# An earlier or later place for the time kernel's turns, the expert loads, the rank products and the token list of a two-layer mixture kernel

## The chip, the cores and the metric

One core of a Trainium2 chip runs the kernel. The metric is the device time of one execution in microseconds; each version is run several times, and the median is given. The engines are TensorE (PE; PEld is its weight load), VectorE (DVE), ScalarE (ACT), GpSimd (POOL) and SyncE (SP), which here only issues loads and stores. DMA is the 16 engines that move the data.

## What is computed

The input `x` is 32 x 32 x 512, that is 1,024 tokens of 512 numbers, in f32. There are two layers, each with a residual:

```python
x = x + ffn0(mix0(x))       # mix0: 32x32 channel matrix, picked per batch entry from 16
x = x + ffn1(conv1(x))      # conv1: a long convolution per channel, masked by length

def ffn0(xt):               # 16 experts, 2 per token, and a shared one of twice the width
    scores = softmax(xt @ router_w + router_b) + router_bias
    ...                     # best 2 of 4 groups, then best 2 experts
    y = sum over experts of gate * ((silu(xt @ ew1 + eb1) * (xt @ ew2 + eb2)) @ ew3 + eb3)
    z = (silu(xt @ sw1 + sb1) * (xt @ sw2 + sb2)) @ sw3 + sb3
    return y + z

def conv1(u):               # the kernel of 512 taps per channel comes from log_dt, C, A
    K = 2 * Re(Cs @ exp(dtA * arange(512)))
    ...
def ffn1(h):                # relu(h @ up)**2 @ down, plus a latent path scaled by the top-2 gate logits
    ...                     # (h @ fc1) @ expert_w, times the sum of the two best logits, @ fc2
    return layernorm(...)
```

The change lies in the first layer, before its expert blocks. Two things of the second layer are prepared there: the rows from which the convolution's kernel (the time kernel) is made, and `expert_w`, turned by TensorE into `ewt`.

## The kernel before

The kernel is written engine by engine; each engine's instructions run in the order written, and semaphores join them. Products that need f32 accuracy are made of three fp32r products of high and low parts (`split3`, L413 to L420): `ah` and `al` hold the mixed tokens, `swh` and `swl` the shared expert's weights.

**Mixing** (PE L1395 to L1413). For each of 8 tiles of 128 tokens PE makes a mixing product, ACT copies it to `xstage` (L692, and every second tile it issues a store to `xrow` in DRAM), PE turns it (L1371), ACT copies the turned tile to `ah` (L734) and DVE the rest to `al` (L919). From tile 4 on, every second tile, PE adds a piece of the router's logits (L1389). Ahead of product 2 PE makes four small turns of the time kernel's rows (L1399, into bank 7), which wait for `s4_in`, four small loads of which `sdt` is the last; they raise `tr_done`. ACT in the same loop takes the exponential of `sdt` (L725, at i == 0) and copies and exponentiates the turned rows (L729 and L732, at i == 1). POOL waits for these, makes five small steps, and then casts the second half of the shared weights (L587, `split_hi(1)`), which DVE splits later (L915).

**Loads** (SP L445 to L486). SP issues in order the tokens, the small loads, the shared weights, then, after `tr_done`, `ewraw` (`expert_w`; it lies where the time kernel's rows lay), and the weights of eight experts (`static_pair` 0 to 3: three loads of 512 KB each, twelve in all). A further pair and `fcraw`, `fc2raw` follow when the mixing is over and `xrow` is stored.

**Shared products and routing** (PE L1502 to L1535). PE makes eight shared products of 12 matmuls each, in four pairs. After pair 0 it waits for `ewraw`, turns it (L1511), and waits until ACT has copied it to `ewt`. Meanwhile DVE works out the routing mask from the logits (L936 to L966). Before the second product of pair 1 the rank products (L1448, L1449) wait for that mask. DVE then works out each token's place in an expert's block and from that two sets of one-hot rows, `hotb` and `hotp` (L1031 to L1037). The last shared product (L1468) is interleaved with 24 small list products of them (L1474, L1477), two behind each of its 12 matmuls; the first 16 give the tokens of each block (`tokx`, L1052), the other 8 their places. POOL gathers the blocks' tokens with them (L622).

**Blocks.** After eight products for a bias (`b3_term`) the 31 expert blocks follow: turn the gathered tokens (L1525), two products with the expert's weights (L1561), one back (L1531). Behind them come the combination, the convolution and the second layer.

Of the kernel before, what the change touches and what calls it, by code (L numbers as in the profile page):

```python
# [27 lines left out]
P = 128  # L28
# [10 lines left out]
def adaln_ffn_program(nc, x, cond, length, cond_w, router_w, router_b, router_bias, ew1, eb1, ew2, eb2, ew3, eb3,  # L39
# [4 lines left out]
    NT = N // P  # L44
    KC = T // P
    BT = P // C
    HALF = N // 2
    TH = NT // 2
    E, _, INTER = ew1.shape
    SH = sw1.shape[1] // INTER  # L50
    G = SH + E
    K = 2
# [22 lines left out]
    YS = 4  # L75
    HOLD = 3
    WARM = 2
    XGS = 4
    AHEAD = 7
    YOS = 4  # L80
# [10 lines left out]
    CBANK = (7, 0, 1, 6)  # L91
# [30 lines left out]
    ah = at(main, "ah", [P, KC, N], F32R)  # L122
    al = at(main, "al", [P, KC, N], F32R)
# [6 lines left out]
    swh = at(exp_reg, "swh", [P, 2, SCOLS], F32R)  # L130
    swl = at(exp_reg, "swl", [P, 2, SCOLS], F32R)
# [181 lines left out]
    bank = [nc.alloc_psum_tensor(f"bank{i}", [P, 512], F32) for i in range(8)]  # L313
# [10 lines left out]
    st_in = [sem(f"st_in{k}") for k in range(4)]  # L324
# [4 lines left out]
    wraw_in, wall_done, wbd2_ok = sem("wraw_in"), sem("wall_done"), sem("wbd2_ok")  # L329
# [21 lines left out]
    a_done, c_done, y_done = sem("a_done"), sem("c_done"), sem("y_done")  # L351
# [8 lines left out]
    b12_ok, ewt_ok = sem("b12_ok"), sem("ewt_ok")  # L360
# [52 lines left out]
    def split3(pe, dst, lhs, rhs, n_k, start=True, stop=True):  # L413

        for k in range(n_k):
            (lh, ll), (rh, rl) = lhs(k), rhs(k)
            pe.matmul(dst, lh, rh, start=(start and k == 0), stop=False)  # L417
            pe.matmul(dst, lh, rl, start=False, stop=False)  # L418
            mm = pe.matmul(dst, ll, rh, start=False, stop=(stop and k == n_k - 1))  # L419
        return mm  # L420
# [20 lines left out]
    def _(sp):  # L441
# [27 lines left out]
        def static_pair(g, landed):  # L469

            dst = ew[:, 2 * g:2 * g + 2, :]
            for src, col in ((ew1, W1), (ew2, W2)):
                sp.dma_start(dst[:, :, col:col + KC * P],
                             src[2 * g:2 * g + 2].rearrange("e (p k) m -> p e (k m)", p=P)).then_inc(landed, 16)
            sp.dma_start(dst[:, :, W3], ew3[2 * g:2 * g + 2].rearrange("e p n -> p e n")).then_inc(landed, 16)

        sp.wait_ge(tr_done, 1)
        sp.dma_start(ewraw[:, :, :], expert_w.rearrange("(a p) m -> p a m", p=P)).then_inc(ew_in, 16)
        for g in range(4):
            static_pair(g, st_in[g // 2])  # L480
        sp.wait_ge(mix_done, NT)
        for par in range(2):
            sp.wait_ge(xrow_out[par], 16 * NT // 4)
# [29 lines left out]
        for n in range(NB):  # L513
# [9 lines left out]
            if n in TOEP_STEPS:  # L523
                g = TOEP_STEPS.index(n)
# [154 lines left out]
    def _(act):  # L679
# [38 lines left out]
        for i in range(NT):  # L718
            if i + 1 < NT:
                x_row(i + 1)  # L720
            if i == 0:
                act.wait_ge(s4_in, 64)
                for a in range(2):
                    s = slice(a * HN, (a + 1) * HN)
                    act.activation(sw[s, 1, :], sdt[s, a::2], ACT.Exp).then_inc(exps_ok, 1)  # L725
            if i == 1:

                act.wait_ge(tr_done, 1)
                act.activation(spar[:, :, :], bank[7][:, 0:4 * HT].rearrange("p (k h) -> p k h", k=4), ACT.Copy)\  # L729
                    .then_inc(spar_ok, 1)  # L730
                act.wait_ge(spar_ok, 1)
                act.activation(sw[:, 0, :], spar[:, 0, :], ACT.Exp).then_inc(exps_ok, 1)  # L732
            act.wait_ge(mix_done, i + 1)
            act.activation(ah[:, :, i * P:(i + 1) * P], bank[2 * (i % 3)][:, :].rearrange("p (k n) -> p k n", k=KC), ACT.Copy)\  # L734
                .then_inc(ah_ok, 1)
            if i >= 4 and i % 2 == 0:
                ltr_copy(i // 2 - 2)
# [615 lines left out]
    def _(pe):  # L1353
# [7 lines left out]
        for w in (6, 7):  # L1361
            for b in range(BT):
                mm = pe.matmul(bank[w][b * C:(b + 1) * C, :], ident[0:C, 0:C],
                               wraw[:, :, :].rearrange("c k d -> c (k d)"), start=True, stop=True)
# [26 lines left out]
            mm.then_inc(lgt_done, 1)  # L1391

        for i in range(NT):
            if i == 2:

                pe.wait_ge(wbd2_ok, BT * len(ACT_TILES))
                pe.wait_ge(s4_in, 64)
                for k, src in enumerate((sstage[:, 0, :], sstage[:, 1, :], cstage[:, :, 0], cstage[:, :, 1])):
                    mm = pe.transpose(bank[7][:, k * HT:(k + 1) * HT], src, ident[0:HT, 0:HT])  # L1399
                mm.then_inc(tr_done, 1)  # L1400
            if i in ACT_TILES:
                pe.wait_ge(wbd2_ok, BT * (ACT_TILES.index(i) + 1))
            else:
                pe.wait_ge(wbd_ok, 1 + BT * (DVE_TILES.index(i) + 1))
            pe.wait_ge(x_in[i // 2], 16)
            wait(pe, xst_ok, i - 2)
            pe.matmul(bank[2 * (i % 3) + 1][:, :], wbd[:, i, :], acc[:, i, :], start=True, stop=True)\  # L1407
                .then_inc(mixr_done, 1)
            if i:
                transpose_mixed(i - 1)  # L1410
            if i >= 4 and i % 2 == 0:
                router_logits(i // 2 - 2)
# [4 lines left out]
        for k in range(2):  # L1417
            mm = pe.transpose(bank[3][:, k * G:(k + 1) * G], bstage[:, k, :], ident[0:G, 0:G])
# [24 lines left out]
        def rank_products():  # L1443

            pe.wait_ge(const_ok, TRI)
            pe.wait_ge(msk_ok, 1)
            wm = w2t[:, :, :].rearrange("p i e -> p (i e)")
            pe.matmul(bank[2][:, 0:NT * E], tri[:, :], wm, start=True, stop=True)  # L1448
            pe.matmul(bank[2][:, NT * E:2 * NT * E], ones[:, :], wm, start=True, stop=True).then_inc(rank_done, 1)  # L1449

        def gates_turned(j):

            pe.wait_ge(silu_ok, 3 + j)
            for i in range(j * TH, (j + 1) * TH):
                mm = pe.transpose(bank[4 + j][0:G, i % TH * P:(i % TH + 1) * P], gates[:, :, i], ident[:, :])
            mm.then_inc(gt_done, 1)

        def last_product():

            gates_turned(0)  # L1460
            pe.wait_ge(b12_ok, 1)
            n = 0
            for k in range(KC):
                lo = k * SH * P + P
                weight, weight_low = swh[:, 1, lo:lo + P], swl[:, 1, lo:lo + P]
                tok, tok_low = ah[:, k, HALF:N], al[:, k, HALF:N]
                for lhs, rhs in ((weight, tok), (weight, tok_low), (weight_low, tok)):
                    mm = pe.matmul(bank[CBANK[3]][:, :], lhs, rhs, start=(n == 0), stop=(n == 3 * K * NT // 2 - 2))  # L1468
                    if n == 3 * K * NT // 2 - 2:
                        mm.then_inc(c_done, 1)  # L1470
                    for m in range(n, n + 2):
                        if m < K * NT:
                            pe.wait_ge(hot_ok, K + m // NT + 1)
                            mm = pe.matmul(bank[3][:, 0:NSLOT], hotp[:, m, :], hotb[:, m, 0, :], start=(m == 0),  # L1474
                                           stop=(m == K * NT - 1))
                        else:
                            mm = pe.matmul(bank[2][:, 0:NSLOT], hotp[:, m - NT, :], hotb[:, m - NT, 1, :],  # L1477
                                           start=(m == K * NT), stop=(m == 3 * NT - 1))
                        if m in (K * NT - 1, 3 * NT - 1):
                            mm.then_inc(tok_done, 1)  # L1480
                    n += 2
                    if n == NT:
                        gates_turned(1)

        def shared_products(u):

            tok = slice(u // 2 * HALF, (u // 2 + 1) * HALF)
            part = u % 2
            for n, sem_done, dst in ((0, a_done, 4 + u % 2), (1, c_done, CBANK[u])):
                pe.wait_ge(swh_ok, n + 1)  # L1490
                pe.wait_ge(swl_ok, n + 1)
                if n == 0:
                    wait(pe, silu_ok, u - 1)
                if n == 0 and u == 1:
                    pe.wait_ge(soft_in, 1)
                if n == 1 and u == 1:
                    rank_products()
                if n == 1 and u == 3:
                    last_product()
                    continue  # L1500
                split3(pe, bank[dst][:, :],
                       lambda k: (swh[:, n, k * SH * P + part * P:k * SH * P + (part + 1) * P],  # L1502
                                  swl[:, n, k * SH * P + part * P:k * SH * P + (part + 1) * P]),
                       lambda k: (ah[:, k, tok], al[:, k, tok]), KC).then_inc(sem_done, 1)
# [6 lines left out]
                mm = pe.transpose(bank[0][:, m * LAT + l * P:m * LAT + (l + 1) * P],  # L1511
                                  ewraw[:, l, m * P:(m + 1) * P], ident[:, :])
        mm.then_inc(tr_done, 1)
        pe.wait_ge(ewt_ok, 1)
        shared_products(1)

        shared_products(2)
# [241 lines left out]
```

## Time and profile before

| | us |
|---|---|
| median of 3 runs | 347.64 |
| lowest, highest | 346.77, 349.14 |
| the profiled execution, its own time | 347.7 |
| its span, first to last instruction | 345.7 |

| engine | busy us | share of the span |
|---|---|---|
| PE | 321.8 | 93% |
| PEld | 243.8 | 71% |
| DVE | 187.4 | 54% |
| ACT | 115.1 | 33% |
| POOL | 108.4 | 31% |

The time lies 2.0 us above the span. Busy time is an average over stages; what an edit is worth is read from the stage where it stands, from the start of each instruction and from what ended the idle time before it. The granted clock is TensorE's alone, 1.00 for 2.4 GHz and 0.50 for 1.2 GHz. L-numbers are lines of the kernel before.

### The profile page before, as it was taken

The numbers are of one execution on the slowest core, as the hardware profiler recorded it, in microseconds if no ns is written. First come the engines' busy times: TensorE is split into PE (matmuls) and PEld (weight loads), VectorE is DVE, ScalarE is ACT, GpSimd is POOL, SyncE is SP. The second block draws the span as 40 slices with busy tenths as digits, with TensorE's granted clock in tenths as the row PEclk, the third lists the DMA queues.
The fourth block names the chain that finished last, engine by engine and source line by source line (L and its number), as shares of the span: only waits on it lengthen the run. The fifth ranks groups of instructions, "written<-read, shape, count | busy, mean of one in ns | idle before, by whom it ended". The sixth has DMA issues, their size and how long they took to land.

```text
span 345.7 us, 5496 instructions
## 1 busy us (share of the span) xinstructions
PE 321.8 (93%) x1945; PEld 243.8 (71%) x1945; DVE 187.4 (54%) x375; ACT 115.1 (33%) x198; POOL 108.4 (31%) x131
## 2 busy tenths in 40 slices
PE   7699899999999899999997997999998999999992
PEld 2367688988887688886864443578887787888871
DVE  4637896889366233454594378346212356433266
ACT  2462312233832232541045633732213333212210
POOL 8350002547477776643200000998000000000000
PEclk9699999999999999999999899999999999999998
DMA  6999900697677789999688990000000000100002
GB/s 194 365 394 404 379 27 0 199 322 225 186 242 219 219 299 327 335 350 409 240 313 344 332 350 6 3 0 0 2 0 0 3 0 30 63 30 2 0 16 105
DMA packets 32830, 59.93 MB, mean 173 GB/s; under 512 B 7213, under 2 KB 8081, under 8 KB 32804
## 3 DMA queue, kind: packets, MB, share of 16 engines
q1 hardware_dynamic: 25764, 48.95, 40.4%
q0 software_dynamic: 4992, 8.42, 7.0%
q10 hardware_dynamic: 2048, 2.21, 1.8%
q8 instruction: 16, 0.26, 0.3%
q14 instruction: 10, 0.08, 0.1%
HBM read 55.02 MB, written 12.40 MB: 195 GB/s over the span
## 4 chain that ended last, share of the span: by engine, by line
PE 71%; DVE 9%; DMA 9%; issue 4%; POOL 2%; ACT 2%; SPq 1%; ACTq 0%; DVEq 0%; POOLq 0%
PE bank L1561 13%; PE bank L417 12%; PE bank L419 12%; PE bank L418 12%; PE bank L1531 6%; DMA toep<-kpad 4%; PE bank L1525 3%; PE bank L1632 2%; DMA sdt<-in_L_cond_log_dt 2%; PE bank L1407 2%; DMA yg<-ytok 2%; DVE acc L1232 2%; DMA xg<-xrow,tokx 1%; PE bank L1468 1%; PE bank L1439 1%
## 5 line engine op out<-in xcount | busy, mean ns | idle before, releaser
L1561 PE MATMUL bank<-xt,ew 128*128 128x128 f32 x496 | 60.7, 276 | 0.0
L1561 PEld LDWEIGHTS bank<-xt,ew 128*128 128x128 f32 x496 | 58.0, 192 | 0.7 <-issue 0.5
L622 POOL DMA_INDIRECT xg<-xrow,tokx x31 | 33.2, 1070 | 43.5 <-DVE tokx L1052 31.1
L629 POOL DMA_INDIRECT ytok<-yout,dstx x31 | 31.8, 1027 | 27.0 <-DVE yout L1164 19.4
L1316 DVE TENSOR_TENSOR sq<-rel 128x512 f32<-128x512 f32 x16 | 13.3, 834 | 43.4 <-ACT rel L863 43.4
L1531 PE MATMUL bank<-ew,bhid 128*128 128x512 f32 x62 | 31.6, 595 | 0.0
L775 ACT ACTIVATE xt<-bank 128x512 f32<-128x512 f32 x31 | 18.4, 597 | 33.5 <-PE bank L1525 33.4
L417 PE MATMUL bank<-dnh,sqh 128*128 128x512 f32 x64 | 25.2, 393 | 1.7 <-DVE sql L1324 1.6
L1525 PEld LDWEIGHTS bank<-ident,xg 128*128 128x128 f32 x124 | 15.1, 141 | 16.5 <-issue 12.7
L669 POOL TENSOR_TENSOR dnl<-dnraw,dnh 128x512 fp32r<-128x512 f32 x8 | 10.5, 1356 | 48.9 <-ACT dnh L830 48.9
L417 PE MATMUL bank<-ah,uph 128*128 128x512 f32 x64 | 25.1, 393 | 0.0
L418 PE MATMUL bank<-dnl,sqh 128*128 128x512 f32 x64 | 24.9, 390 | 0.0
L419 PE MATMUL bank<-dnh,sql 128*128 128x512 f32 x64 | 24.9, 390 | 0.0
L419 PE MATMUL bank<-ah,upl 128*128 128x512 f32 x64 | 24.9, 389 | 0.0
L418 PE MATMUL bank<-al,uph 128*128 128x512 f32 x64 | 24.9, 389 | 0.0
L1164 DVE COPY yout<-bank 128x512 f32<-128x512 f32 x31 | 21.4, 690 | 2.8 <-PE bank L1531 0.6
L1632 PE MATMUL bank<-toep,u_t 128*32 128x512 f32 (+3 forms) x256 | 20.4, 466 | 2.7 <-DMA toep<-kpad 1.6
L863 ACT ACTIVATE rel<-bank 128x512 f32<-128x512 f32 x16 | 9.6, 599 | 36.8 <-PE bank L419 36.7
L1173 DVE SCALAR_TENSOR_TENSOR bhid<-bank,b12d,bsil 128x128 f32<-128x128 f32 x15 | 5.3, 351 | 27.6 <-ACT bsil L787 27.6
L1525 PE MATMUL bank<-ident,xg 128*128 128x128 f32 x124 | 18.6, 274 | 1.4 <-DMA xg<-xrow,tokx 1.4
L1632 PEld LDWEIGHTS bank<-toep,u_t 128*32 128x32 f32 x256 | 8.1, 116 | 14.3 <-issue 10.0
L1324 DVE TENSOR_TENSOR sql<-sq,sqh 128x512 fp32r<-128x512 f32 x16 | 12.0, 750 | 9.8 <-PE bank L419 5.6
(315 smaller groups left out, 611.3 us busy)
## 6 DMA issues: line engine op xcount, KB each, us to landing
ew<-in_L_ffn_ew SPq DMA_DIRECT2D x51, 256.0 KB, 3.7
ew<-in_L_ffn_ew SPq DMA_DIRECT2D x21, 512.0 KB, 10.6
toep<-kpad SPq DMA_DIRECT2D x4, 1536.0 KB, 12.7
yg<-ytok SPq DMA_DIRECT2D x8, 512.0 KB, 3.9
acc<-in_x SPq DMA_DIRECT2D x4, 512.0 KB, 7.4
xrow<-xstage ACTq DMA_DIRECT2D x4, 512.0 KB, 6.8
upraw<-in_L_ffn_up_w SPq DMA_DIRECT2D x1, 2048.0 KB, 10.1
dnraw<-in_L_ffn_down_w SPq DMA_DIRECT2D x1, 2048.0 KB, 16.4
```

Of the source, the lines that this page charges most:

```text
L417: pe.matmul(dst, lh, rh, start=(start and k == 0), stop=False)
L418: pe.matmul(dst, lh, rl, start=False, stop=False)
L419: mm = pe.matmul(dst, ll, rh, start=False, stop=(stop and k == n_k - 1))
L622: pool.indirect_dma_start(xg[:, n % XGS, :], None, xrow, bass.IndirectOffsetOnAxis(ap=tokx[:, n:n + 1].bitcast(U32), axis=0), bounds_check ...
L629: pool.indirect_dma_start(ytok, bass.IndirectOffsetOnAxis(ap=dstx[:, n:n + 1].bitcast(U32), axis=0), yout[:, n % YOS, :], None, bounds_che ...
L775: act.activation(xt[:, n % 2, :, :], bank[n % 2][:, :].rearrange("p (k n) -> p k n", k=KC), ACT.Copy)\
L1164: dve.tensor_copy(yout[:, n % YOS, :], bank[6 + n % 2][:, :]).then_inc(yout_ok, 1)
L1316: tt(sq[:, v % 2, :], rel[:, v % 2, :], rel[:, v % 2, :], ALU.mult).then_inc(sq_ok, 1)
L1525: mm = pe.transpose(bank[n % 2][:, k * P:(k + 1) * P], xg[:, n % XGS, k * P:(k + 1) * P], ident[:, :])
L1531: pe.matmul(bank[6 + n % 2][:, :], bhid[:, n % BHS, :], ew[:, ring(n), W3], start=True, stop=True)\
L1561: mm = pe.matmul(bank[2 + n % 2][:, w * P:(w + 1) * P], ew[:, ring(n), col + k * P:col + (k + 1) * P], xt[:, n % 2, k, :], start=(k == 0), ...
L1632: mm = pe.matmul(bank[g % 3][j * B:(j + 1) * B, 0:T - k * P], u_t[:, h0 + j, k, :], toep[:, (h0 + j) % TS, k * P:T], start=(k == 0), stop= ...
```

## The change

Five edits, all ahead of the expert blocks:

- PE's four turns of the time kernel's rows stand ahead of mixing product 4 (the fifth) instead of 2; ACT's two steps on them move from i == 0 and 1 to i == 3 and 4.
- SP issues the twelve expert loads ahead of `ewraw`, after `wall_done` (they overwrite the matrices that the first products read), and `ewraw` after them, still behind `tr_done`.
- PE waits for `ewt` ahead of the second product of pair 1, not ahead of the first.
- The rank products stand after the first three matmuls of that product (`middle_product`) instead of ahead of it.
- The list products come four behind each of the last shared product's first six matmuls instead of two behind each of twelve.

```diff
@@ SP
+        sp.wait_ge(wall_done, 2)
+        for g in range(4):
+            static_pair(g, st_in[g // 2])
         sp.wait_ge(tr_done, 1)
         sp.dma_start(ewraw[:, :, :], expert_w.rearrange("(a p) m -> p a m", p=P)).then_inc(ew_in, 16)
-        for g in range(4):
-            static_pair(g, st_in[g // 2])
@@ ACT, mixing loop
-            if i == 0:
+            if i == 3:
                 act.wait_ge(s4_in, 64)
...
-            if i == 1:
+            if i == 4:
 
                 act.wait_ge(tr_done, 1)
@@ PE, mixing loop
         for i in range(NT):
-            if i == 2:
+            if i == 4:
@@ PE
+        def middle_product():
...
+            split3(pe, bank[CBANK[1]][:, :], weights, tokens, 1, stop=False)
+            rank_products()
+            split3(pe, bank[CBANK[1]][:, :], lambda k: weights(k + 1), lambda k: tokens(k + 1), KC - 1, start=False)\
+                .then_inc(c_done, 1)
@@ PE, last_product
-                    for m in range(n, n + 2):
+                    for _ in range(LIST_STEP if m < 3 * NT else 0):
...
-                    n += 2
-                    if n == NT:
+                    if n == 4:
                         gates_turned(1)
@@ PE, shared_products
                 if n == 1 and u == 1:
-                    rank_products()
+                    pe.wait_ge(ewt_ok, 1)
+                    middle_product()
+                    continue
@@ PE, before shared_products(1)
         mm.then_inc(tr_done, 1)
-        pe.wait_ge(ewt_ok, 1)
         shared_products(1)
```

`LIST_STEP` is 4. In `last_product` the counters are renamed, so that `n` counts matmuls and `m` list products; the second four turns of the gates still stand behind its fourth matmul.

## Rows read from the trace of the kernel before

**Rows 1.** The page: engine, busy us (share of the span), instructions.
```profile
span 345.7 us, 5496 instructions
PE 321.8 (93%) x1945; PEld 243.8 (71%) x1945; DVE 187.4 (54%) x375; ACT 115.1 (33%) x198; POOL 108.4 (31%) x131
```

**Rows 2.** The chain that ended last, 0 to 66 us: start, us, what.
```profile
4.87 7.51 DMA sdt<-in_L_cond_log_dt
...
13.10 2.00 PE bank L1407 x2
...
18.52 0.90 PE bank L1407 x2
```

**Rows 3.** Timeline of the mixing: start, us, engine, line, what [idle before <-releaser].
```profile
9.03 0.64 PE L1371 MATMUL bank<-ident,xstage 128*128 128x128 f32 x4
...
10.40 0.58 ACT L692 ACTIVATE xstage<-bank 128x512 f32<-128x512 f32 x1
...
12.52 0.36 PE L1399 MATMUL bank<-ident,sstage 16*128 16x16 f32 x2 [2.85 <-DMA sdt<-in_L_cond_log_dt]
...
17.54 1.04 POOL L587 CAST swh<-swraw 128x1024 fp32r<-128x1024 f32 x1
...
28.21 1.22 DVE L915 TENSOR_TENSOR swl<-swraw,swh 128x1024 fp32r<-128x1024 f32 x1
```

**Rows 4.** Windows: stretch, its length, busy of each engine, clock, DMA share, GB/s.
```profile
12.52:18.49 5.97, 5.97 (x17) 3.65 (x18) 1.91 (x4) 2.92 (x8) 3.03 (x7) 0.50 1.07 368
12.52:39.60 27.08, 25.39 (x125) 18.17 (x126) 16.42 (x46) 12.55 (x27) 6.63 (x20) 0.89 1.06 391
185.77:188.75 2.98, 0.66 (x6) 0.43 (x5) 1.11 (x2) 1.43 (x2) 0.00 (x0) 1.00 1.01 409
189.15:192.56 3.41, 3.41 (x32) 1.40 (x28) 0.00 (x0) 1.99 (x3) 0.00 (x0) 0.50 1.04 400
```

**Rows 5.** Timeline around the turns of ewraw and the rank products.
```profile
35.82 0.60 PE L1511 MATMUL bank<-ident,ewraw 128*128 128x128 f32 x4
...
37.10 0.50 PE L417 MATMUL bank<-ah,swh 128*128 128x512 f32 x1 [0.69 <-ACT ewt L747]
...
40.76 0.46 PE L1448 MATMUL bank<-w2t,tri 128*128 128x128 f32 x2 [0.64 <-DVE w2t L966]
```

**Rows 6.** The chain that ended last, from the list products to the first block.
```profile
52.79 0.23 PE bank L1468
53.02 0.13 PE bank L1474 x2
53.15 0.33 PE bank L1468
...
62.71 0.87 PE bank L1525 x8
...
64.96 1.11 PE bank L1561 x10
```

**Rows 7.** Timeline of SP's queue.
```profile
11.84 0.64 SPq L467 DMA_DIRECT2D drow<-in_L_cond_D  x1
13.13 0.39 SPq L478 DMA_DIRECT2D ewraw<-in_L_ffn_expert_w  x1
...
25.99 1.71 SPq L475 DMA_DIRECT2D ew<-in_L_ffn_ew  x1
34.02 0.88 SPq L473 DMA_DIRECT2D ew<-in_L_ffn_ew  x2
```

**Rows 8.** DMA issues at 13.13, 25.99 and 34.02: KB, us to landing.
```profile
ewraw<-in_L_ffn_expert_w SPq DMA_DIRECT2D x1, 256.0 KB, 5.9
...
ew<-in_L_ffn_ew SPq DMA_DIRECT2D x1, 512.0 KB, 13.6
...
ew<-in_L_ffn_ew SPq DMA_DIRECT2D x1, 512.0 KB, 5.4
```

**Rows 9.** Timeline of DVE: the second set of one-hot rows.
```profile
49.33 2.35 DVE L1037 TENSOR_TENSOR hotp<-srem,prow 128x1024 fp32r<-128x1024 f32 x2
```

More of the change, by code:

```diff
@@ L77, in adaln_ffn_program @@
     WARM = 2
+    LIST_STEP = 4
     XGS = 4
@@ L1449, in rank_products, with weights, tokens @@
             pe.matmul(bank[2][:, NT * E:2 * NT * E], ones[:, :], wm, start=True, stop=True).then_inc(rank_done, 1)
+        def middle_product():
+            def weights(k):
+                lo = k * SH * P + P
+                return swh[:, 1, lo:lo + P], swl[:, 1, lo:lo + P]
+            def tokens(k):
+                return ah[:, k, 0:HALF], al[:, k, 0:HALF]
+            split3(pe, bank[CBANK[1]][:, :], weights, tokens, 1, stop=False)
+            rank_products()
+            split3(pe, bank[CBANK[1]][:, :], lambda k: weights(k + 1), lambda k: tokens(k + 1), KC - 1, start=False)\
+                .then_inc(c_done, 1)
         def gates_turned(j):
@@ L1461, in last_product @@
             pe.wait_ge(b12_ok, 1)
-            n = 0
+            n = m = 0
             for k in range(KC):
@@ L1467, in last_product @@
                 for lhs, rhs in ((weight, tok), (weight, tok_low), (weight_low, tok)):
-                    mm = pe.matmul(bank[CBANK[3]][:, :], lhs, rhs, start=(n == 0), stop=(n == 3 * K * NT // 2 - 2))
-                    if n == 3 * K * NT // 2 - 2:
+                    mm = pe.matmul(bank[CBANK[3]][:, :], lhs, rhs, start=(n == 0), stop=(n == 3 * KC - 1))
+                    n += 1
+                    if n == 3 * KC:
                         mm.then_inc(c_done, 1)
-                    for m in range(n, n + 2):
+                    for _ in range(LIST_STEP if m < 3 * NT else 0):
                         if m < K * NT:
@@ L1478, in last_product @@
                                            start=(m == K * NT), stop=(m == 3 * NT - 1))
-                        if m in (K * NT - 1, 3 * NT - 1):
+                        m += 1
+                        if m in (K * NT, 3 * NT):
                             mm.then_inc(tok_done, 1)
-                    n += 2
-                    if n == NT:
+                    if n == 4:
                         gates_turned(1)
```

## The prediction

> **What bounds the kernel now.** I read the page first: TensorE (PE) is busy 93% of the span, so a change pays only where PE waits, works at half clock, or gets other work [rows 1]. The change touches the time up to the expert blocks, so I then read the chain of work that ended last for the first 66 us. It runs through the load of `sdt`, which lands at 4.87 + 7.51 = 12.38, and then through PE: four small transposes of the time kernel's rows, then mixing product 2 at 13.10 [rows 2]. The timeline shows PE with nothing to do between 9.67 and 12.5, put down to that load [rows 3]. The windows add the clock: from 12.52 to 18.49 it was 0.50, which is 1.2 of 2.4 GHz, and a mixing product then took 2.00 instead of the 0.90 us that one took from 18.52 on [rows 2, 4].
>
> After that PE is the chain nearly without a hole. There are two: 0.69 us for the copy of the turned expert matrix (`ewt`) and 0.64 us for the routing mask [rows 5]. The first expert block starts at 64.96 [rows 6]. I take everything behind it as moved along unchanged, because every later load, gather and copy is released by the blocks before it; this is the assumption with the widest reach.
>
> **The change, part by part.**
>
> *Time kernel's turns at the fifth product.* PE no longer waits for `sdt` before product 2. The gap of 2.8 us goes, and with it probably the cause of the low clock: PE was busy all through the 5.97 us at half clock, half of which, 3.0, is loss [rows 3, 4]. At most 5.8 us. ACT gives some back: its second mixing copy waits until 10.40 behind the copy that needs the router's bias [rows 3]. I take 4.5 (between 2.8 and 5.8). The s4 rows have landed at 12.38, before the fifth product comes up. ACT's exponentials, and with them POOL's five small steps and second weight cast, come a few us later against the mixing; DVE splits that cast only at 28.21, almost 10 us after POOL has ended it at 18.58, so this is hidden [rows 3]. Without that cover it would cost at most the 2 us or so by which the cast is late.
>
> So PE would end the first shared pair not at 35.82 [rows 5] but at about 31.3 (30.0 to 33.0).
>
> *Expert loads first, `ewraw` behind them.* This is what decides. SP's queue now: the last small load ends at 11.84 + 0.64 = 12.48, `ewraw` is issued at 13.13, and the twelve expert loads of 512 KB from 13.5 to 25.99 + 1.71 = 27.70 [rows 7]. `ewraw` landed 5.9 us after its issue, at 19.0; the last of the twelve 13.6 us after its own, at 25.99 + 13.6 = 39.6 [rows 8]. The DMA engines are busy throughout: their share is 1.06 in the mean from 12.52 to 39.60 [rows 4]. So starting the loads one microsecond earlier (12.5 instead of 13.5) brings nothing, they already wait for bandwidth; and the bytes up to the end of the thirteen loads are the same in either order. The order decides only who is last, and now it is `ewraw`, a quarter megabyte that PE needs between its first and second shared pair. I put its landing where the last of the thirteen lands now, 39.6 (39.2, if a little slack is found; 40.2, if its shorter rows take longer; as a far bound 27.7 + 13.6 = 41.3, a full queue's delay behind an issue at the end of the twelve). On SP's queue `tr_done` is long there by then, and the loads behind `ewraw` (the seventh pair, `fcraw`, `fc2raw`) are issued from 34.02 now [rows 7]; they are needed in the blocks or later, and wait longer today for the stores of the mixed rows.
>
> Queued behind the wait on PE is everything: the four turns, `tr_done`, the rest of the shared products. ACT stands too, since its copy into `ewt` waits for the turns and its SiLU copies come after. DVE goes on alone: the routing mask, on which the rank products start at 40.76 now [rows 5], is done 4.5 us earlier, at about 36, and then DVE waits for PE.
>
> A load issued later can finish before an earlier one: the first one issued at 34.0 landed 5.4 us on, at 39.5, about level with the twelfth [rows 8]. The Trainium skill, "DMA: Bandwidth & Descriptors", section "Queues, rings and completion order", says that each DMA engine takes descriptors in ring order, but that completion over a load's engines is not first in, first out; the trace agrees, with 39.5 against 39.6, and by the strict order the time below is 351.8, by overtaking of that size 351.7.
>
> *What the wait does to the clock.* PE would stand from about 31.3 to 39.6, 8 us, where now a gap of 2.8 us brought half clock for 6.0 us of work behind it, and a stretch of 3.0 us in which PE was busy for 0.66 us brought it for 3.4 us at 189 [rows 3, 4]. Half of what runs at that clock is loss: 1.7 to 3.0 us. I take 2.2, nearer the shorter, because dense 512-column products follow here as they did at 189. Below, none, if the clock is back before PE is; above, 3.0. Mixing itself no longer runs at half clock, but that gain is already in the 4.5 us, and it ends in the wait.
>
> *`ewt` wait moved, rank products inside.* The 12 products of the second pair's first half now run while ACT copies `ewt`: the gap of 0.69 us goes. Three products stand before the rank products, and the mask is long there: 0.64 us goes [rows 5]. Together 1.33. That needs the mask, not PE, to be early, which the late `ewraw` makes sure of; in the rival where `ewraw` is early, the three products (3 x 0.23 us) still cover it. DVE's work behind the rank products is not the bound: `hotp`, its last step for the list, ends at 51.68, and PE begins its list only at 53.02; with 9 instead of 12 products between, some 0.7 us of that distance goes [rows 6, 9]. If it were gone altogether, the wait would be put down to `hotp` and cost under 1 us.
>
> *List, four per step.* A product behind list products costs 0.33 us, behind another product 0.23, a pair of list products 0.13 [rows 6]. The 24 list products stay; the steps fall from 12 to 6, so six crossings at 0.10 go: 0.6 us. The tokens come a good us earlier, but PE did not wait for the first gather at 62.71 [rows 6], so that is worth nothing now. The bounds are 0 (if the crossing price returns inside the list) and 0.8.
>
> *The sum.* From the start of the turns to the first block PE now takes 64.96 - 35.82 = 29.14 us, of which 1.33 are waits; without them and the 0.6 it is 27.2. Afterwards it starts at 39.6: 39.6 + 27.2 = 66.8, and with 2.2 for the clock 69.0, which is 4.1 us later than 64.96. The span goes from 345.7 to 349.8; the profiled execution's own time was 347.7, 2.0 more than its span, and equal to the median of 347.64. So 347.7 + 4.1 = 351.8 us.
>
> **The rivals.**
>
> *The late load, but a cheap clock.* If the clock is back within 2 us of PE's return, its loss is 0 to 1: the time is 1.9 to 2.9 us longer, 349.6 to 350.6, within 1%. For it: 3.4 us was enough at 189. Against: 6.0 us at 12.5 [rows 4].
>
> *`ewraw` gets through: faster.* If the queue is not what holds a load but only its own size, it lands as `ewraw` did, 5.9 us after an issue at some 27 to 28, at about 33.1. PE waits under 2 us, keeps its clock, and reaches the block at 33.1 + 27.2 = 60.3, 4.7 earlier: 343.0. The mask at 36 still comes before the rank products at 33.1 + 4.3 = 37.4. It decides from a landing before 37.7 (64.96 - 27.2) on. For it: 5.9 and 5.4 us stand in the rows. Against: the load issued into the full queue took 13.6, and at 27 it is full [rows 7, 8].
>
> *Still later.* A landing at 41.3 with 3.0 for the clock: 41.3 + 27.2 + 3.0 - 64.96 = 6.5, so 354.2.
>
> *The gain of the front is not there.* If ACT, not `sdt`, held the mixing, PE would still end the first pair at 35.8 and wait from there to 39.6; the time is the same 351.8, since the landing sets it.
>
> **How the numbers follow.** The late load with its clock price 0.58; cheap clock 0.20; early `ewraw` 0.14; still later 0.08. A measurement of this kernel tells about 1%, 3.5 us, from no change; of the first case a tenth lies under that. So slower 0.52 + 0.08 = 0.60, within 1% 0.20 + 0.06 = 0.26, faster 0.14. The range has the first two cases, most of the fourth, and 1 us for the spread of the runs below: 348.6 to 354.0. The likeliest case alone spans 347.7 + 3.2 (39.2, 1.7) to + 5.5 (40.2, 3.0): 350.9 to 353.2.
>
> **What would show it.** Right: no wait for `sdt` on PE, clock 1.00 from 12 to 19 us; the turns of `ewraw` start near 39.6 after an idle of 6 to 9 us put down to that load; its time to landing is over 10 us; half clock behind it; no waits for `ewt` or `w2t`; first block at 68 to 70. Wrong: turns before 37, or a load of `ewraw` that lands within 6 us of its issue; a first block before 65 would mean a gain. A stretch behind the first block whose length changes by over 1 us would break the assumption that the rest only moves.

## The result and the profile after

| | before | changed |
|---|---|---|
| median us (4 runs each) | 347.2 | 352.39 |
| lowest, highest | 346.2, 349.14 | 350.77, 353.38 |
| profiled execution, its own time | 347.7 | 350.77 |
| its span | 345.7 | 348.8 |

The ratio is 1.0127, 95% interval 1.0080 to 1.0174: slower by about 1.3% (the medians differ by 1.5%). A ratio counts only the runs within 1.5% of the fastest of their kernel, a median counts all. 352.39 lies 0.6 from the forecast 351.8 and inside its range. The profiled execution is the fastest of the four; the other three are 1.6 to 2.6 us longer, with a mean granted clock of 0.974 against its 0.981, and no profile shows where they lost it. The page of the changed kernel, first its span, then each engine's busy us (share), instructions:

```profile
span 348.8 us, 5495 instructions
PE 320.5 (92%) x1945; PEld 243.4 (70%) x1945; DVE 187.5 (54%) x375; ACT 114.9 (33%) x198; POOL 109.6 (31%) x131
```

PE is busy 1.3 us less than before [rows 1] and the span is 3.1 us longer: PE waits more. The timeline of PE tells where (start, us, engine, line, what, idle before and its releaser; L1401 are the four turns of the time kernel's rows, L1530 those of `ewraw`, L1450 the rank products):

```profile
12.18 0.66 PE L1373 MATMUL bank<-ident,xstage 128*128 128x128 f32 x4
12.77 0.29 PE L1401 MATMUL bank<-ident,sstage 16*128 16x16 f32 x2
...
30.80 0.39 PE L420 MATMUL bank<-ah,swl 128*128 128x512 f32 x1
39.34 1.11 PE L1530 MATMUL bank<-ident,ewraw 128*128 128x128 f32 x4 [8.15 <-DMA ewraw<-in_L_ffn_expert_w]
40.11 0.78 PE L418 MATMUL bank<-ah,swh 128*128 128x512 f32 x1
...
44.64 0.38 PE L1450 MATMUL bank<-w2t,tri 128*128 128x128 f32 x2
```

The small turns no longer wait for `sdt` [rows 3]. The first shared pair ends at 31.2 instead of 35.8 [rows 5], 4.6 us earlier. Then PE stands 8.15 us. The waits for `ewt` and for the mask are gone [rows 5]. SP's queue and the load's time to landing (last row; KB, us):

```profile
11.49 0.64 SPq L468 DMA_DIRECT2D drow<-in_L_cond_D  x1
12.17 1.02 SPq L474 DMA_DIRECT2D ew<-in_L_ffn_ew  x2
...
27.23 1.24 SPq L476 DMA_DIRECT2D ew<-in_L_ffn_ew  x1
28.51 1.17 SPq L482 DMA_DIRECT2D ewraw<-in_L_ffn_expert_w  x1
```

```profile
ewraw<-in_L_ffn_expert_w SPq DMA_DIRECT2D x1, 256.0 KB, 10.8
```

`ewraw` is issued at 28.51 instead of 13.13 [rows 7] and lands 10.8 us later, at 39.3, where the last of the thirteen loads landed before (39.6) [rows 8]. The windows (length, busy us of PE, PEld, DVE, ACT, POOL, clock, DMA share, GB/s):

```profile
12.50:18.50 6.00, 6.00 (x37) 4.12 (x35) 3.11 (x6) 4.10 (x11) 1.26 (x2) 1.00 1.06 378
31.20:39.30 8.10, 0.00 (x0) 0.00 (x0) 4.53 (x16) 0.00 (x0) 0.00 (x0) 0.76 1.06 384
39.34:42.31 2.97, 2.97 (x9) 2.57 (x10) 0.00 (x0) 1.80 (x2) 0.00 (x0) 0.50 1.07 371
42.31:45.00 2.69, 2.69 (x15) 2.24 (x14) 0.75 (x1) 1.46 (x3) 0.00 (x0) 1.00 0.54 194
```

The mixing now runs at full clock, where it ran at half [rows 4]; while PE waits the clock falls, and the first 2.97 us of its work afterwards run at 0.50. The DMA share is 1.06, as before. The first expert block starts at 68.10 on the chain, 3.14 us after the 64.96 of before [rows 6], and behind it both kernels take the same: 280.8 and 280.9 us from PE's first block product to the end of the span. In this pair of profiles the whole loss lies ahead of the blocks.

### The profile page after: what moved, and what is told of

Its sections match the earlier page's. It is cut to its first block, busy times and chain, and to the rows that moved or that the text cites. A ratio compares the mean times of both kernels' runs of the same rounds, so it can differ in the third digit from the quotient of the medians.

```text
span 348.8 us, 5495 instructions
## 1 busy us (share of the span) xinstructions
PE 320.5 (92%) x1945; PEld 243.4 (70%) x1945; DVE 187.5 (54%) x375; ACT 114.9 (33%) x198; POOL 109.6 (31%) x131
## 4 chain that ended last, share of the span: by engine, by line
PE 65%; DMA 12%; SPq 8%; DVE 6%; issue 5%; POOL 2%; ACT 1%; DVEq 0%; POOLq 0%; ACTq 0%
PE bank L1579 13%; PE bank L418 12%; PE bank L419 11%; PE bank L420 11%; PE bank L1549 6%; DMA toep<-kpad 4%; PE bank L1543 3%; DMA ewraw<-in_L_ffn_expert_w 3%; SPq L474 3%; DMA yg<-ytok 3%; PE bank L1650 2%; SPq L476 2%; DVE acc L1234 2%; DMA xg<-xrow,tokx 1%; PE bank L1441 1%
## 5 line engine op out<-in xcount | busy, mean ns | idle before, releaser
L418 PE MATMUL bank<-ah,uph 128*128 128x512 f32 x64 | 25.1, 392 | 0.1
L1650 PE MATMUL bank<-toep,u_t 128*32 128x512 f32 (+3 forms) x256 | 20.4, 466 | 2.4 <-DMA toep<-kpad 1.3
```

The source lines that it names most:

```text
L1650: mm = pe.matmul(bank[g % 3][j * B:(j + 1) * B, 0:T - k * P], u_t[:, h0 + j, k, :], toep[:, (h0 + j) % TS, k * P:T], start=(k == 0), stop= ...
```

## The experiments

The theory: the time is set by where `ewraw` lands, a place that only its position in SP's queue decides, plus a price for the clock behind the wait. The rivals: one of the other edits costs; or full DMA engines hold any load that long.

The table is read from PE's timeline in each kernel's profile: the start of the turns of `ewraw`, of the first list product and of the first block product, then two distances and the rest of the span, in us. "Start" is the time that the 16 first products of PE (the channel matrices) take: 1.9 after what is called a quick start below, 3.6 after a slow one; more on that at the last experiment.

| kernel | start | turns | list | first block | turns to block | rest |
|---|---|---|---|---|---|---|
| before | 1.9 | 35.82 | 52.86 | 64.80 | 28.98 | 280.9 |
| changed | 1.9 | 39.34 | 55.97 | 67.94 | 28.60 | 280.8 |
| order undone | 3.6 | 34.48 | 50.85 | 62.81 | 28.33 | 283.7 |
| order alone | 3.6 | 39.58 | 59.04 | 71.00 | 31.42 | 284.9 |
| filler | 1.9 | 39.52 | 54.77 | 66.70 | 27.18 | 284.4 |
| `ewraw` seventh | 1.9 | 31.21 | 47.58 | 59.51 | 28.30 | 282.3 |
| `ewraw` on ACT's queue | 3.6 | 34.58 | 50.93 | 62.89 | 28.31 | 281.6 |
| list by two | 3.6 | 34.37 | 50.71 | 62.76 | 28.39 | 283.0 |
| rank products back | 3.6 | 34.21 | 51.26 | 63.19 | 28.98 | 282.8 |
| turns back | 3.6 | 34.28 | 50.63 | 62.59 | 28.31 | 282.0 |
| before, again | 1.9 | 32.87 | 49.92 | 61.87 | 29.00 | 280.7 |
| changed, again | 2.2 | 39.24 | 56.46 | 68.39 | 29.15 | 280.5 |
| order undone, again | 1.9 | 31.38 | 47.76 | 59.69 | 28.31 | 284.0 |
| turns back, again | 3.6 | 34.02 | 50.37 | 62.33 | 28.31 | 284.8 |

### Order undone: `ewraw` first again, the other edits kept

```diff
-        sp.wait_ge(wall_done, 2)
-        for g in range(4):
-            static_pair(g, st_in[g // 2])
         sp.wait_ge(tr_done, 1)
         sp.dma_start(ewraw[:, :, :], expert_w.rearrange("(a p) m -> p a m", p=P)).then_inc(ew_in, 16)
+        for g in range(4):
+            static_pair(g, st_in[g // 2])
```

> The changed kernel with the order of SP's loads undone alone: ewraw first, then the twelve expert loads. Theory (the late landing of ewraw is the whole loss, and the clock behind it): ewraw lands near 19 to 20, PE goes on at 31.0 without a wait, the mask is ready at about 36 and is waited for under 1 us, the first block starts at 59 to 60 and the time is 341 to 343, 5 to 6 us under the kernel before and 10 under the changed one. Rival (another of the edits costs: the rank products inside, the list of four, the later turns): the time stays at or above that of the kernel before, 347 or more.

Measured: a median of 345.62 us (10 runs, 341.39 to 348.52), against 347.4 of before (19 runs beside it). The medians differ by 0.5%; the ratio is 0.9885, 0.9835 to 0.9935, and counts six of the ten runs, whose median is 343.5. The median of the changed kernel, 352.39, is 6.8 us higher. Against before that is less than expected in size. The profile, of the slowest of the ten, shows what can hold it back: this execution started slowly, its turns begin at 34.48, not 31; and its rest is 283.7, 2.8 more than in the profiles of before. The direction is that of the theory: with the order undone the other edits together are a gain. PE does not wait for `ewraw` here, but for the mask:

```profile
39.41 0.46 PE L1449 MATMUL bank<-w2t,tri 128*128 128x128 f32 x2 [0.91 <-DVE w2t L967]
```

The second profile (below) has the early turns.

### Order alone: the kernel before, its twelve expert loads put first

```diff
+        sp.wait_ge(wall_done, 2)
+        for g in range(4):
+            static_pair(g, st_in[g // 2])
         sp.wait_ge(tr_done, 1)
         sp.dma_start(ewraw[:, :, :], expert_w.rearrange("(a p) m -> p a m", p=P)).then_inc(ew_in, 16)
-        for g in range(4):
-            static_pair(g, st_in[g // 2])
```

> The kernel before with the order of SP's loads alone changed: the twelve expert loads first, ewraw behind them; nothing else. Theory: PE ends the first shared pair at about 36, ewraw lands at 39.3, so PE stands 3.3 us; the wait for the mask goes (0.64), that for ewt stays (0.69); with 0 to 3 us for the clock the time is 2.7 to 5.7 us above the kernel before, 350 to 353. That is as slow as the whole change, although the front has gained nothing. Rival (the loss is in the other edits): 347 to 348.

Measured: 353.73 us (4 runs, 349.56 to 357.86), ratio 1.0134, 1.0043 to 1.0224. That is about the loss of all the changes together, without one of the others. PE's wait in the timeline, and the windows behind it (the profile is of the longest run, 357.86):

```profile
39.58 1.12 PE L1512 MATMUL bank<-ident,ewraw 128*128 128x128 f32 x4 [5.50 <-DMA ewraw<-in_L_ffn_expert_w]
```

```profile
39.58:47.38 7.80, 7.11 (x21) 5.55 (x21) 0.75 (x1) 3.05 (x4) 0.00 (x0) 0.50 0.60 211
47.38:50.00 2.62, 2.62 (x14) 2.16 (x14) 1.94 (x12) 0.21 (x1) 0.00 (x0) 1.00 0.00 0
```

The landing is the same within 0.2 us, 39.5, though the front is that of before. The order alone makes the loss. The low clock lasts 7.8 us here, against 2.97 in the profile of the changed kernel.

### Filler: PE kept busy while it waits

```diff
+        for _ in range(34):
+            pe.matmul(bank[0][:, :], swh[:, 0, 0:P], ah[:, 0, 0:HALF], start=True, stop=True)
         pe.wait_ge(ew_in, 16)
```

> The changed kernel with 34 more matmuls of 512 columns (about 7.8 us, into a bank that the turns overwrite) between the first shared pair and the wait for ewraw; their results are not used. Theory (the idle costs clock, beside the wait): the turns still start near 39.3, the granted clock stays 1.00 there, and the first block comes 1.5 to 3 us earlier, near 66.5; the time is 349 to 350.5, against 351 to 353 of the changed kernel. Rival (the low clock costs nothing because something else bounds there): the time of the changed kernel.

Measured: 354.06 us (4 runs, 349.91 to 355.45). The time did not fall as expected. The mechanism did what it should; timeline of PE, then the windows:

```profile
31.46 7.87 PE L1529 MATMUL bank<-ah,swh 128*128 128x512 f32 x34
39.52 0.66 PE L1533 MATMUL bank<-ident,ewraw 128*128 128x128 f32 x4 [0.18 <-DMA ewraw<-in_L_ffn_expert_w]
```

```profile
31.20:39.30 8.10, 8.10 (x36) 6.38 (x35) 4.92 (x18) 0.00 (x0) 0.00 (x0) 1.00 1.06 384
39.50:45.00 5.50, 5.48 (x28) 4.70 (x29) 1.50 (x6) 3.26 (x4) 0.00 (x0) 1.00 0.82 285
```

The clock stays at 1.00 and from the turns to the first block PE takes 27.18 us, against 28.60 and 29.15 in the two profiles of the changed kernel. There the clock was low for 2.97 and 4.24 us of work, half of which is 1.5 and 2.1: 27.18 + 1.5 = 28.7 and 27.18 + 2.1 = 29.3, each within 0.2 of what was measured. So the clock's price is shown ahead of the blocks. It did not reach the time: in this execution the rest took 284.4 us, 3.6 more than in those two profiles. What takes that time is treated under "what the runs showed of the hardware"; that the filler causes it isn't shown, the same lengthening stands in kernels without it.

### `ewraw` as the seventh load

```diff
-        for g in range(4):
+        for g in range(2):
             static_pair(g, st_in[g // 2])
         sp.wait_ge(tr_done, 1)
         sp.dma_start(ewraw[:, :, :], expert_w.rearrange("(a p) m -> p a m", p=P)).then_inc(ew_in, 16)
+        for g in range(2, 4):
+            static_pair(g, st_in[g // 2])
```

> The changed kernel with ewraw issued between the sixth and the seventh expert load. Theory (a load lands when what was queued ahead of it on SP's queue has landed): ewraw lands where the sixth does now, at 30 to 31, so PE waits under 1 us, and the time is that of the kernel with ewraw first within 1 us, 341 to 343. Rival (the landing is set by the length of the queue as a whole, not by the place in it): ewraw lands after 36 and the time is 347 or more.

Measured: 345.52 us (10 runs, 343.83 to 348.94), ratio 0.9967, 0.9923 to 1.0012. Issue on SP's queue, and KB and time to landing:

```profile
17.24 1.15 SPq L482 DMA_DIRECT2D ewraw<-in_L_ffn_expert_w  x1
```

```profile
ewraw<-in_L_ffn_expert_w SPq DMA_DIRECT2D x1, 256.0 KB, 13.4
```

It lands at 17.24 + 13.4 = 30.6, where the theory put it. PE's turns begin at 31.21 without a wait. The place in the queue decides, in three steps: ahead of the twelve 18.2 to 21.0 us, behind six 30.6, behind twelve 39.2 to 39.5. In time this kernel is not told from that with `ewraw` first, nor with certainty from before; 341 to 343 was too low: the profiled run, the fastest of the ten at 343.83, has a rest of 282.3, 1.4 more than before, and what held the others back was not profiled.

### `ewraw` on ACT's queue

```diff
@@ SP
-        sp.wait_ge(tr_done, 1)
-        sp.dma_start(ewraw[:, :, :], expert_w.rearrange("(a p) m -> p a m", p=P)).then_inc(ew_in, 16)
@@ ACT, i == 4
                 act.activation(sw[:, 0, :], spar[:, 0, :], ACT.Exp).then_inc(exps_ok, 1)
+                act.dma_start(ewraw[:, :, :], expert_w.rearrange("(a p) m -> p a m", p=P)).then_inc(ew_in, 16)
```

> The changed kernel with the twelve expert loads first on SP's queue, as changed, but ewraw issued on ACT's queue, right after its copies of the time kernel's rows (near 18 us). Theory (ewraw is late because it stands behind the twelve in one queue, not because the DMA engines are full): it lands under 8 us after its issue, before 26, although the engines are as busy as before; PE does not wait for it, the turns start near 31 and the first block at 59 to 60. Rival (full engines hold any load for 11 us or more): it lands after 29, and with the bytes of the twelve ahead of it at 36 to 39; the first block comes at 65 or later.

Measured: 345.82 us (6 runs, 343.88 to 347.0), ratio 0.9917, 0.9882 to 0.9952. The load:

```profile
ewraw<-in_L_ffn_expert_w ACTq DMA_DIRECT2D x1, 256.0 KB, 9.4
```

A miss for both in its numbers: issued at 21.14, it lands at 30.5, later than the 26 expected and past the rival's 29, but well ahead of 36 to 39. So the twelve loads in SP's queue do not bind it as they do in that queue, but with the engines full and a store of `xrow` ahead of it in its own queue (20.46) 256 KB still take 9.4 us; which of the two sets that was not tested. PE, at 34.58, did not wait for it.

### The list by two again

`LIST_STEP = 2` in place of 4, on the kernel with the order undone.

> The kernel with SP's order undone and the other edits kept, its list products again two per step (LIST_STEP 2). Theory: six more crossings at 0.10 us, so from the start of the list products to the first block 0.6 us more than with four per step; nothing else moves ahead of the list. Rival (four in a row cost PE as much as two and two): no difference in that distance.

Measured: 347.67 us in one run, too few to tell a time. From the first list product to the first block 12.05 us, with four per step 11.93 to 11.97. That is 0.1 us, not 0.6, and even this is not the list's: the kernel before and the order alone, which have two per step as well, take 11.94 to 11.96. The list by two loses its 0.1 ahead of the second turns of the gates, which start 0.25 us behind the fourth pair (52.07 to 52.32) and 0.14 in the kernel before (54.22 to 54.36). So four per step gain nothing. The chains of the changed kernel and of this one, from a matmul of the last shared product on:

```profile
56.13 0.35 PE bank L1491 x4
56.48 0.32 PE bank L1484
```

```profile
50.87 0.13 PE bank L1490 x2
51.00 0.33 PE bank L1483
```

The crossing costs the same 0.1, and there are half as many, but the third and fourth list product in a row cost 0.11 each, not 0.065: two cost 0.13, four 0.35. What the crossings give back, these take. Each list product has its own 128 x 128 weights for 32 columns, and PEld is busy 0.42 us with the weights of two and 0.65 us with those of four, 0.11 to 0.12 more for each; that the weights set the pace fits this, but no run tests it.

### The rank products and the wait for `ewt` back

```diff
                 if n == 1 and u == 1:
-                    pe.wait_ge(ewt_ok, 1)
-                    middle_product()
-                    continue
+                    rank_products()
...
         mm.then_inc(tr_done, 1)
+        pe.wait_ge(ewt_ok, 1)
         shared_products(1)
```

> The kernel with SP's order undone and the other edits kept, but the wait for ewt again ahead of the second shared pair and the rank products again ahead of that pair's second product. Theory: the turns start near 31 as with the edit; PE waits 0.7 for ewt and under 0.5 for the mask, and 12 instead of 9 products stand between the rank products and the list, so the list begins about 0.7 us later. Rival: the edit gave nothing or cost, the list begins at the same time or earlier.

Measured: 348.01 us in one run. From the turns to the list 17.05 us, against 16.34 to 16.38 with the edit. The edit is worth 0.7 us, as expected, when the mask is the last to come: the rank products then start at the same distance from the turns (4.94 and 4.93 us), with three products ahead of them instead of behind.

### Turns back, and four kernels profiled again

The kernel with the order undone and the turns of the time kernel's rows back ahead of product 2 (`if i == 2` on PE, `i == 0` and `i == 1` on ACT):

> The kernel with SP's order undone and the rank and list edits kept, but the time kernel's turns back ahead of the third mixing product, and ACT's steps on them at i == 0 and 1. Theory (the later turns give the front 4 to 5 us): PE waits for sdt again near 10 to 12.5, its clock is 0.50 behind that, the turns of ewraw start near 35.8, the first block at 63.5 to 64.3, some 4 us after the kernel with the later turns. Rival (the mixing is paced by ACT and the loads anyway): the first block at 60 to 61.

346.59 us in one run. The theory fails here: its turns of `ewraw` begin at 34.28, no later than in the four kernels with the later turns that also started slowly (34.21 to 34.58). PE's first products, in the timeline of this kernel:

```profile
5.22 3.64 PE L1364 MATMUL bank<-wraw,ident 32*32 32x512 f32 x16
8.79 3.78 PE L1408 MATMUL bank<-acc,wbd 128*128 128x512 f32 x4
12.37 1.06 PE L1372 MATMUL bank<-ident,xstage 128*128 128x128 f32 x4
13.36 0.39 PE L1400 MATMUL bank<-ident,sstage 16*128 16x16 f32 x2
```

Everything takes twice as long until some 13.5 us, so the first turned tile ends at 13.4, when `sdt` has landed (5.70 + 6.6 = 12.3), and no wait is left for the later turns to remove. To tell the two starts apart, both kernels and both forms of the front were profiled again, with no edit:

> The kernel before, unchanged, profiled again. Two kinds of start were seen: the 16 first products take 1.9 us (full clock from about 5 us) or 3.6 us (half clock until 13 to 14 us). Theory (the front's gain is there only after a quick start): after a quick start the turns of ewraw begin at 35.8, as in the first profile; after a slow one PE has no wait for sdt left, and they begin at 34 to 34.5, earlier than after the quick one. Rival (the slow start costs this kernel as much as the others): 38 to 39 after a slow start.

> The changed kernel, unchanged, profiled again. Theory: whichever way it starts, the turns begin where ewraw lands, 39 to 40, and the first block comes 28.6 us later with the clock low for 3 us of work, up to 30.2 with it low for 6: 67.5 to 70. Rival (the landing moves with the front): after a slow start the turns begin 3 us later, at 42 or more.

> The changed kernel with SP's order undone, profiled again. Theory: after a quick start the turns begin at 31 and the first block comes at 59.5; after a slow start 34.4 and 62.8, as in its first profile. Rival (the first profile's 34.5 is what this order costs, a second late start of the loads for instance): 34 to 35 after a quick start too.

> The same with the time kernel's turns back at their old place, profiled again. Theory: after a quick start PE waits for sdt, and the turns of ewraw begin at 35.5 to 36, 4.5 us after those of the kernel with the later turns; after a slow start 34.3 as in its first profile. Rival (the later turns give nothing in either start): 31 to 32 after a quick start.

Single runs: before 344.35, changed 350.96, order undone 345.62, turns back 348.95. The changed kernel's turns begin at 39.24 and its first block comes at 68.39, as the theory has it. The order undone has its turns at 31.38 after a quick start. Turns back started slowly again (34.02), so its quick start was not seen. The kernel before started quickly and still missed the expectation, at 32.87 instead of 35.8. Timeline, then the windows:

```profile
12.32 0.27 PE L1399 MATMUL bank<-ident,sstage 16*128 16x16 f32 x2 [2.80 <-DMA sdt<-in_L_cond_log_dt]
```

```profile
9.60:12.30 2.70, 0.00 (x0) 0.01 (x1) 2.29 (x14) 0.71 (x3) 0.00 (x0) 1.00 1.09 343
12.40:18.50 6.10, 6.10 (x32) 3.94 (x33) 3.18 (x6) 4.30 (x11) 3.77 (x9) 1.00 1.07 371
```

The wait for `sdt` is there, 2.80 us long, but the clock did not fall behind it. So the front of the kernel before is worth three different times: 35.82 (quick start, clock falls in the wait), 32.87 (quick start, it does not), and 34.0 to 34.3 after a slow start, read from the kernel with the turns back, whose front is the same up to there. The later turns bring it to 31.2 to 31.4 after a quick start and leave 34.2 to 34.6 after a slow one: a gain of 4.5, of 1.5 to 1.7, or of nothing. All three end in the changed kernel's wait for `ewraw`.

## Why the prediction was right

**The late load.** Right, and shown: landing 39.3 (forecast 39.6), idle 8.15 us (8), DMA share 1.06 as before; the expert loads are issued 1.4 us earlier and the last landing moves by 0.3. The order alone makes the loss, its undoing takes it away, and the load moves with its place. Nothing that was issued behind the twelve got ahead of them: the twelfth lands at 27.23 + 11.3 = 38.5, `ewraw` at 39.3, and level with it the next one, issued at 29.80. The two orders of the forecast, 0.1 us apart, are not told apart by the time (34.02 + 5.4 in their working is 39.4, not 39.5).

**The clock behind the wait.** Right in kind, shown by the filler; 1.5 and 2.1 us in two profiles of the changed kernel, forecast 2.2 (1.7 to 3.0), so the first lies under the lower bound. In the order-alone kernel 7.8 us ran at half clock, a bound of 3.9; its 31.42 us from the turns to the block are 3.1 more than the 28.98 of before less the 0.64 for the mask.

**The waits for `ewt` and the mask.** Mis-sized. Forecast 1.33. With the filler, PE's way from the turns to the first list product is 15.25; it was 17.04. So 1.79 went with the two waits, 0.46 more than the idle shown in the rows [rows 5]; that this is the restart behind them is likely, not shown. The prediction also let the three products cover the mask where `ewraw` is early. They do not: in the seven profiles in which PE goes on without a wait for `ewraw` and the rank products stand inside, it waits 0.91 to 0.93 us for the mask. In the changed kernel, with `ewraw` late, that wait is gone, as forecast.

**The list.** Mis-sized. Forecast 0.6, measured nothing (11.94 before, 11.93 with the filler), the lower bound that was given: the price did come back inside the list. The two errors nearly cancel, 0.46 against 0.6, and the 29.14 that they were taken from was 0.16 too long (its end is read from the chain, its start from the timeline, which has 28.98): 27.2 was hit at 27.18 by luck.

**The front.** The 4.5 us were right for the profiled pair (4.6) but only there: it was 1.5 to 1.7 where the clock did not fall in that wait, and nothing after a slow start. The step that failed is "with it probably the cause of the low clock", taken from one profile. It did no harm to the time of the changed kernel, since the landing hides the front; it makes the loss against before larger in the executions whose front was not held up: 39.3 less 32.9, 34.2 or 35.8 is 6.4, 5.1 or 3.5 us. The medians differ by 5.2 us, and the sum had 4.1. That the median lies only 0.6 from the forecast is luck in part: the profiled pair, from which the sum was made, differs by 3.1, 1.0 less than the sum, by 0.3 of the landing and 0.7 of the clock; the other runs of the changed kernel were longer than its profile, and the median of before fell from 347.64 to 347.2 with a fourth run.

**Everything behind only moves.** Right for the four profiles of before and changed (280.5 to 280.9 us). In the ten experiments the rest was 281.6 to 284.9; see below.

## What to carry to other kernels

In a full queue like this one, the place of a load sets its landing time: when loads are pulled ahead, work out what now stands behind them and who needs that first; starting the saturated queue 1.4 us earlier brought its last landing forward by only 0.3. A gain upstream of a wait that a load sets is worth nothing until the load moves, so undo the one edit and keep the others: here that makes 345.62 us out of 352.39. Before pricing a wait's effect on the clock from one profile, look at a second one.

## What the runs showed of the hardware

**Two starts.** In 6 of 14 profiles the 16 first products took 1.9 us, in one 2.2, in seven 3.6, for the same instructions. All seven slow ones were on kernels of the experiments and none of the four on before and changed, but the same code showed both (order undone: 3.6, then 1.9). In the slow starts the granted clock's row still reads 1.00 (window 5.22 to 8.80 of the turns-back kernel), while the durations double; the first record of the clock in those traces comes only at 13 to 14 us. Durations are the safer reading there.

**A wait of 2.8 us lowered the clock once and once not**, in the same kernel.

**The rest of the span** is 280.5 to 284.9 us without an edit there. The convolution takes 24.5 to 25.1 us in five profiles (both of before, both of changed, and `ewraw` on ACT's queue) and 27.3 to 29.0 in the nine others. From its end on all fourteen take 131.8 to 132.0 us. PE's wait for the last load of the convolution's matrices, in the first profiles of before and of order undone:

```profile
208.60 2.36 PE L1632 MATMUL bank<-toep,u_t 128*32 128x512 f32 x32 [1.55 <-DMA toep<-kpad]
207.64 3.91 PE L1649 MATMUL bank<-toep,u_t 128*32 128x512 f32 x32 [4.38 <-DMA toep<-kpad]
```

That load lands 19.2 to 19.8 us after the convolution's first product in the five and 20.4 to 21.6 in the nine. In the nine the clock is low behind this wait (with the rank products back also at the convolution's start), in the five only at the convolution's start or not at all. Why stays open; no run was made on it. Both profiles of order undone and both with the turns back have it long, so it may go with the kernel and not with the execution. It is the reason why order undone again and `ewraw` seventh, whose first block comes 5.1 and 5.3 us earlier than in the first profile of before, show only 2.1 and 3.9 in the time (345.62 and 343.83 against 347.7).

**Small products in a row** (128 x 32, each with new 128 x 128 weights) cost 0.11 us each from the third on, against 0.065 for the first two behind a product of 512 columns.
